# Attention and mixing on one core, eight batches in flight by steps: row units in two groups a step, value products between column units, one dense unit last

## The chip, the cores and the metric

The kernel runs on one core of a Trainium2 chip. The metric is the device time of one execution in microseconds, the median of several; lower is better.

## The reference

The input x is 8 batches of 1024 tokens with 256 channels. Each batch has six modulation vectors sa, ca, ga, sb, cb, gb from a small conditioning input. All is float32.

```
h = layernorm(x) * (1 + ca) + sa
q, k, v = split(h @ w_in.T)                       # 16 heads of 16 channels
a = softmax(causal(q @ k.T / 4)) @ v
x = x + ga * (a @ w_out.T + b_out)
h = layernorm(x) * (1 + cb) + sb
p = h shifted by one token
r = sigmoid((mu_r*h + (1-mu_r)*p) @ W_r.T)
k = relu((mu_k*h + (1-mu_k)*p) @ W_k.T) ** 2
out = x + gb * (r * (k @ W_v.T))
```

## The kernel before

Products that need float32 accuracy are made of a high and a low part (`o_hi`, `o_lo` and so on; three matmuls for one). Queries and keys are split into three bfloat16 parts that lie stacked in the partitions of `q_stack` and `k_stack`, one pair of stacks for even and one for odd groups of heads.

**Batches, quarters, steps.** A batch `b` has G = 4 quarters `s` of 4 heads, a quarter has 12 steps `t`. Three parts of three batches run beside one another: the attention of batch b, the front of batch b+1 (layernorm, transposes, q, k and v) and the back of batch b-1 (everything behind the attention, 256 tokens a quarter). `body(b, kind)` is written once for each engine; kinds are first (only a front), start, second, mid (a loop), last and drain (only backs). `timeline` yields for each step the back items `(b, s, u)`, where u is the stage number from 0 to `BACK_END`-1; a stage past 11 falls in the next quarter. In the drain a quarter's back starts `TAIL_LAG` = 5 steps after the one before it. Each engine runs its own program in order and waits on semaphores.

**Column units.** `score_columns` makes transposed scores, keys in the partitions, of one key tile against up to 512 queries; a unit fills one of 3 banks `col_ps`, and ScalarE's `exps` turns it into `weights`. A quarter has 38 of them: 4, 4, 2, 1, 4, 4, 4, 4, 4, 4, 2, 1 by step. On the steps with the diagonal (0 to 3 and 8 to 11) GpSimd's `select` zeroes the masked part. `values` multiplies the weights of step t with `v_ones`; TensorE does it in step t+1.

**Row units.** The exponent needs each query's maximum beforehand. `row_unit` makes the scores of the next group of heads with queries in the partitions, in one of 3 banks `row_ps`, and VectorE's `maximum` reduces it. A quarter has 38 row units and, at two points, a transpose of the split maxima (`mt0` for the first half of the queries, `MT1` for the second), which SyncE copies into a row of `q_stack`. `PER_STEP` says how many units of `ORDER` a step has. The first 11 need the first half of the next stack, the others its second half; SyncE's `fill_stacks` writes these with 6 DMAs a side. The second half's query side is released by the last column unit of the quarter before, its key side comes after `place_values` (which waits for ScalarE's `val_out` copy) and the three DMAs of MT1's maxima.

**Dense units.** All other products share a single bank `dense_ps`: v, qk and transposed (front), and out, norm, recept, key and value (back). `V_STEPS`, `QK_STEPS`, `T_STEPS` and `BACK_STEPS` say on which step TensorE runs each. `claim_dense` lets the next one start when the one before has been taken out of the bank (semaphores `free[...]`): v, transposed, norm, recept and key by ScalarE, out and value by VectorE, qk by both.

**Order within a step, before.** TensorE: column units, then (at step 0) MT1 of the quarter before, the value product of the step before, the front unit, the back units; the row units are spread among them by `rows_after`, in proportion to a weight of 1 to 4 for columns, 4 for a value product and 6 for a dense unit. VectorE: a fifth of the maxima, back items, front items, three fifths of the maxima, `rest_of_qk`, a fifth of the maxima. ScalarE: half of the exps, back items, the other exps, copies of `val_ps`, front unit. GpSimd: select, front, back.

The back's stages before, by engine: att_n (VectorE 0), o_hi (ScalarE 1), the residual add and o_lo (GpSimd 1), out (TensorE 2), gated and x1 (VectorE 3), stats (4), rstd (GpSimd 4), xn_c (VectorE 5), norm (TensorE 5), h (ScalarE 6), h_diff (GpSimd 6), mixed (VectorE 7), mix_hi (ScalarE 8), mix_lo (GpSimd 8), recept and key (TensorE 9 and 10, emptied by ScalarE at 10 and 11), k_hi (ScalarE 11), k_lo (GpSimd 11), value (TensorE 13), mix_out (VectorE 14), the output's two adds and its DMA (GpSimd 14).

## Time and profile before

| | |
|---|---|
| median of 3 runs | 1716.88 us (1710.48 to 1721.14) |
| the profiled execution | 1714.77 us |
| its span | 1713.2 us |
| TensorE matmuls (PE) | busy 1425.7 us, 83% of the span |
| VectorE (DVE) | 1183.1 us, 69% |
| ScalarE (ACT) | 910.8 us, 53% |
| GpSimd (POOL) | 738.0 us, 43% |
| mean granted TensorE clock | 0.958 of full speed |

The span lies within the execution's time, 1.6 us of which is around it. PEld is TensorE's loading of weights, which overlaps its matmuls; SPq is SyncE's DMA queue. A matmul's end is modelled, so a busy TensorE is not one at its peak. Idle time of an engine is put down to what released it last; "issue" means that the profile shows no releaser.

### The profile page before, as it was taken

The numbers are of one execution on the slowest core, as the hardware profiler recorded it, in microseconds if no ns is written. First come the engines' busy times: TensorE is split into PE (matmuls) and PEld (weight loads), VectorE is DVE, ScalarE is ACT, GpSimd is POOL, SyncE is SP. The second block draws the span as 40 slices with busy tenths as digits, with TensorE's granted clock in tenths as the row PEclk, the third lists the DMA queues.
The fourth block names the chain that finished last, engine by engine and source line by source line (L and its number), as shares of the span: only waits on it lengthen the run. The fifth ranks groups of instructions, "written<-read, shape, count | busy, mean of one in ns | idle before, by whom it ended". The sixth has DMA issues, their size and how long they took to land.

```text
span 1713.2 us, 33031 instructions
## 1 busy us (share of the span) xinstructions
PE 1425.7 (83%) x10024; PEld 749.3 (44%) x10024; DVE 1183.1 (69%) x2306; ACT 910.8 (53%) x1795; POOL 738.0 (43%) x878
## 2 busy tenths in 40 slices
PE   3698999788988988788897888879888898899755
PEld 2253444344544444444443445434454444444344
DVE  4768767877677776877578675777767777777232
ACT  2057555556555555565455555565545655566521
POOL 3223314444354434455344443545435553444554
PEclk9899999999999999999999999999999999999855
DMA  3211131111311122111311113111221112111200
GB/s 105 63 62 52 49 105 57 38 54 55 104 57 47 49 72 85 43 53 57 93 55 48 45 57 96 64 42 45 72 86 56 55 49 78 47 61 40 71 19 19
DMA packets 101874, 103.00 MB, mean 60 GB/s; under 512 B 21296, under 2 KB 89912, under 8 KB 101696
## 3 DMA queue, kind: packets, MB, share of 16 engines
q1 hardware_dynamic: 98176, 91.59, 16.6%
q0 software_dynamic: 2560, 8.39, 1.3%
q8 instruction: 94, 1.54, 0.4%
q10 hardware_dynamic: 960, 0.79, 0.2%
q14 instruction: 84, 0.69, 0.1%
HBM read 31.74 MB, written 8.94 MB: 24 GB/s over the span
## 4 chain that ended last, share of the span: by engine, by line
PE 47%; DVE 21%; issue 12%; ACT 9%; POOL 6%; SPq 2%; DMA 2%; DVEq 1%; ACTq 0%; POOLq 0%
PE row_ps L1076 9%; PE val_ps L1100 9%; PE col_ps L1046 7%; PE dense_ps L1110 7%; DVE max_a L871 7%; PE dense_ps L1112 5%; PE dense_ps L1111 5%; ACT weights L715 4%; DVE mixed L984 3%; DVE max_b L871 2%; PE row_ps L1081 2%; PE dense_ps L1129 2%; DVE xn_c L910 2%; DVE gated L968 1%; SPq L459 1%
## 5 line engine op out<-in xcount | busy, mean ns | idle before, releaser
L715 ACT ACTIVATE weights<-col_ps 128x512 f32<-128x512 f32 (+1 forms) x1216 | 620.6, 580 | 471.1 <-PE col_ps L1046 469.1
L871 DVE TENSOR_REDUCE max_a<-row_ps 128x1 f32<-128x512 f32 (+3 forms) x864 | 550.3, 663 | 224.7 <-PE row_ps L1081 145.4
L1076 PE MATMUL row_ps<-k_stack,q_stack 125*128 125x512 bf16 (+3 forms) x1536 | 460.5, 337 | 54.7 <-DVE max_a L871 35.3
L1046 PE MATMUL col_ps<-q_stack,k_stack 128*128 128x512 bf16 (+3 forms) x1536 | 393.9, 333 | 57.1 <-ACT weights L715 36.0
L597 POOL TENSOR_SCALAR_AFFINE_SELECT weights<-weights 128x512 f32<-128x512 f32 x256 | 169.5, 662 | 533.0 <-ACT weights L715 531.1
L1100 PE MATMUL val_ps<-weights,v_ones 128*32 128x512 f32 (+3 forms) x3072 | 329.5, 501 | 16.4 <-POOL weights L597 15.6
L1076 PEld LDWEIGHTS row_ps<-k_stack,q_stack 125*128 125x128 bf16 x1536 | 144.9, 99 | 348.8 <-DVE max_a L871 173.0
L871 DVE TENSOR_REDUCE max_b<-row_ps 128x1 f32<-128x384 f32 (+3 forms) x352 | 213.1, 635 | 107.3 <-PE row_ps L1081 106.9
L1046 PEld LDWEIGHTS col_ps<-q_stack,k_stack 128*128 128x128 bf16 x1536 | 131.9, 98 | 220.8 <-ACT weights L715 138.8
L1081 PE MATMUL row_ps<-causal,ident_bf 128*128 128x128 bf16 x1024 | 203.6, 224 | 0.0
L1081 PEld LDWEIGHTS row_ps<-causal,ident_bf 128*128 128x128 bf16 x1024 | 102.9, 100 | 14.3
L1100 PEld LDWEIGHTS val_ps<-weights,v_ones 128*32 128x32 f32 x3072 | 60.8, 108 | 109.4 <-issue 66.1
L984 DVE SCALAR_TENSOR_TENSOR mixed<-h_diff,mus,h 128x256 f32<-128x256 f32 x128 | 76.2, 654 | 21.8 <-POOL h_diff L652 21.7
L659 POOL TENSOR_TENSOR mix_lo<-mixed,mix_hi 128x512 fp32r<-128x512 f32 x64 | 81.4, 1291 | 6.8 <-ACT mix_hi L782 6.8
L652 POOL TENSOR_TENSOR h_diff<-h 128x512 f32<-128x512 f32 x32 | 33.3, 1039 | 92.9 <-ACT h L774 92.2
L1110 PE MATMUL dense_ps<-h_hi,w_hi 128*128 128x512 f32 x128 | 60.8, 475 | 7.9 <-DVE qk_rest L942 4.2
L1110 PE MATMUL dense_ps<-w_hi,o_hi 128*128 128x256 f32 x128 | 41.2, 322 | 26.7 <-POOL o_lo L638 20.2
L1129 PE MATMUL dense_ps<-ident,xn_c 128*128 128x128 f32 x128 | 22.5, 303 | 47.6 <-DVE xn_c L910 45.5
L723 ACT ACTIVATE val_out<-val_ps 128x512 f32<-128x512 f32 x64 | 38.6, 603 | 30.9 <-PE val_ps L1100 30.7
L1110 PE MATMUL dense_ps<-mix_hi,w_hi 128*128 128x256 f32 x128 | 40.9, 320 | 15.0 <-ACT h_hi L758 12.1
L736 ACT ACTIVATE v_ones<-dense_ps 128x512 f32<-128x512 f32 x32 | 20.1, 629 | 60.5 <-PE dense_ps L1112 60.5
L1112 PE MATMUL dense_ps<-h_hi,w_lo 128*128 128x512 f32 x128 | 51.0, 399 | 0.0
(128 smaller groups left out, 2261.1 us busy)
## 6 DMA issues: line engine op xcount, KB each, us to landing
q_stack<-q_part SPq DMA_DIRECT2D x384, 64.0 KB, 2.5
k_stack<-k_part SPq DMA_DIRECT2D x372, 64.0 KB, 2.5
xa<-in_x SPq DMA_DIRECT2D x8, 1024.0 KB, 6.9
att<-val_out SPq DMA_DIRECT2D x64, 128.0 KB
recips<-recip_rows SPq DMA_DIRECT2D x32, 256.0 KB
xq<-in_x SPq DMA_DIRECT2D x28, 256.0 KB, 3.3
out<-xq POOLq DMA_DIRECT2D x28, 256.0 KB, 2.6
q_stack<-max_rows SPq DMA_DIRECT2D x192, 4.0 KB
```

What stands on the lines that cost most here:

```text
L597: nc.gpsimd.affine_select(out=w, in_=w, compare_op=ALU.is_ge, fill=0.0, base=0, pattern=[[0, G], [1, P]], channel_multiplier=-1).then_inc( ...
L659: nc.gpsimd.tensor_tensor(mix_lo[:, m], mixed[:, m], mix_hi[:, m].bitcast(F32), ALU.subtract).then_inc(mix_lo_done, 1)
L715: nc.scalar.activation(weights[:, t % 2, h:h + n, 0:q1 - q0], col_ps[bank][:, 0:n * (q1 - q0)].rearrange("p (h q) -> p h q", h=n), ACT.Exp ...
L871: nc.vector.reduce_max(dest, bank[:, 0:len(heads) * (k1 - k0)].rearrange("p (h k) -> p h k", h=len(heads)), AX_X).then_inc(max_done, 1)
L984: last = nc.vector.scalar_tensor_tensor(mixed[:, m, c, :], h2_diff[:, c, :], mus[:, m, c:c + 1], h2[s % 2][:, c, 0:QT], ALU.mult, ALU.add)
L1046: last = nc.tensor.matmul(col_ps[bank][:, i * (q1 - q0):(i + 1) * (q1 - q0)], k_stack[s % 2][:, h, P * j:P * (j + 1)], q_stack[s % 2][:, h ...
L1076: last = nc.tensor.matmul(bank[:, n * width:(n + 1) * width], q_stack[stack][0:MAX_AT, h, P * i:P * (i + 1)], k_stack[stack][0:MAX_AT, h, ...
L1081: last = nc.tensor.matmul(bank[:, (n + 1) * width - P:(n + 1) * width], ident_bf[:], causal[:], start=False, stop=end, skip_group_check=True)
L1100: last = nc.tensor.matmul(val_ps[32 * h:32 * h + 32, q0 - base:q1 - base], v_ones[:, j, G * s + h].rearrange("p d a -> p (d a)"), weights[ ...
L1110: nc.tensor.matmul(dst, a_hi(c), b_hi(c), start=(c == 0), stop=False)
L1111: nc.tensor.matmul(dst, a_hi(c), b_lo(c), start=False, stop=False)
L1112: last = nc.tensor.matmul(dst, a_lo(c), b_hi(c), start=False, stop=(c == KC - 1))
```

## The change

- TensorE's step becomes: two row units, half of the column units, the value product of the step before, the other column units, the remaining row units, then the front's and the back's dense unit. MT1 moves from step 0 of the next quarter to the end of step 11. `rows_after` and its weights go.
- `PER_STEP` puts 4, 4, 3, 4, 5, 2, 4, 4, 2, 4, 2, 1 units in the steps instead of 2, 3, 3, 3, 3, 4, 4, 5, 5, 4, 2, 1, and `mt0` stands behind 19 row units instead of 14.
- The front's and the back's units get other steps, so that a step holds one dense unit (two in step 1 of a batch's first quarter). norm, recept and key are one step later.
- ScalarE and VectorE empty the dense bank at the head of the next step, by `empty_dense` (and `front`, `rest_of_qk` with t - 1). What splits a value in a high part comes last in ScalarE's step (`split`). VectorE does one half of mixed before its later maxima and one after; its other back items and the front come last.
- GpSimd does the front and back items of a step ahead of the select; its stages are 2, 5, 8, 10, 13 and 15 instead of 1, 4, 6, 8, 11 and 14. At stage 2 o_lo comes ahead of the residual add. `BACK_END` is 16 instead of 15.

```diff
-PER_STEP = [2, 3, 3, 3, 3, 4, 4, 5, 5, 4, 2, 1]
+PER_STEP = [4, 4, 3, 4, 5, 2, 4, 4, 2, 4, 2, 1]
-V_STEPS, QK_STEPS, T_STEPS = (0, 1, 2, 3), (4, 6, 7, 8), (4, 6, 8, 10)
+V_STEPS, QK_STEPS, T_STEPS = (0, 1, 3, 9), (4, 5, 7, 8), (3, 5, 7, 9)
-BACK_STEPS = dict(zip(BACK_UNITS, (2, 5, 9, 10, 13)))
-BACK_END = 15
+BACK_STEPS = dict(zip(BACK_UNITS, (2, 6, 10, 11, 13)))
+BACK_END = 16
...
+        def row_groups(t):
+            first = sum(PER_STEP[:t])
+            units = list(range(first, first + PER_STEP[t]))
+            return units[:2], units[2:]
...
 # gpsimd
             def body(b, kind):
                 for s, t, at in timeline(b, kind):
-                    if attends(kind) and t in DIAGONAL:
-                        select(b, s, t)
                     front(b, kind, s, t)
                     for item in at:
                         back(*item)
+                    if attends(kind) and t in DIAGONAL:
+                        select(b, s, t)
...
 # scalar
             def body(b, kind):
                 for s, t, at in timeline(b, kind):
-                    units = range(COL_FIRST[t], COL_FIRST[t + 1]) if attends(kind) else ()
-                    for c in units[:len(units) // 2]:
-                        exps(b, s, t, c)
+                    front(b, kind, s, t)
                     for item in at:
-                        back(*item)
-                    for c in units[len(units) // 2:]:
+                        empty_dense(*item)
+                    for c in range(COL_FIRST[t], COL_FIRST[t + 1]) if attends(kind) else ():
                         exps(b, s, t, c)
...
-                    front(b, kind, s, t)
+                    for item in at:
+                        split(*item)
...
 # vector
+                    early, late = row_groups(t) if has_rows(kind, s) else ([], [])
                     if t == 0 and attends(kind):
                         maximum(b, s - 1, MT1)
-                    for u in units[0]:
+                    for u in early[:1]:
+                        maximum(b, s, u)
+                    rest_of_qk(b, kind, s, t)
+                    for item in at:
+                        empty_dense(*item)
+                    for u in early[1:]:
                         maximum(b, s, u)
                     for item in at:
+                        mix(*item, 0)
+                    for u in late:
+                        maximum(b, s, u)
+                    for item in at:
+                        mix(*item, 1)
                         back(*item)
                     front(b, kind, s, t)
-                    for u in units[1] + units[2] + units[3]:
-                        maximum(b, s, u)
-                    rest_of_qk(b, kind, s, t)
-                    for u in units[4]:
-                        maximum(b, s, u)
...
 # tensor
+                    for u in early:
+                        row_unit(b, s, u)
+                    for c in cols[:len(cols) // 2]:
                         score_columns(b, s, t, c)
-                        if t:
-                            rows_after(COL_HEADS[t])
-                    if t == 0 and cols:
-                        row_unit(b, s - 1, MT1)
-                        rows_after(4)
-                    if has_values:
-                        values(*late)
-                        rows_after(4)
+                    if attends(kind) if t else has_late(kind, s):
+                        values(*last)
+                    for c in cols[len(cols) // 2:]:
+                        score_columns(b, s, t, c)
+                    for u in late:
+                        row_unit(b, s, u)
                     if unit:
                         claim_dense()
                         front(unit)
-                        rows_after(6)
-                    for item in backs_now:
-                        claim_dense()
-                        back(*item)
-                        rows_after(6)
-                    rows_after(work)
+                    for item in at:
+                        if back_unit(*item):
+                            claim_dense()
+                            back(*item)
+                    if t == STEPS - 1 and has_rows(kind, s):
+                        row_unit(b, s, MT1)
```

## Rows read from the trace of the kernel before

**Rows 1.** The page, its chain of work that ended last, by engine.

```profile
PE 47%; DVE 21%; issue 12%; ACT 9%; POOL 6%; SPq 2%; DMA 2%; DVEq 1%; ACTq 0%; POOLq 0%
```

**Rows 2.** Busy time by stretch: batch 0, batches 1 to 6, batch 7, drain.

```profile
core 0: us, PE busy (x) PEld busy (x) DVE busy (x) ACT busy (x) POOL busy (x), PEclk, DMA share, GB/s
90.60:246.20 155.60, 143.12 (x1043) 64.18 (x1042) 114.83 (x230) 95.34 (x189) 42.91 (x60) 0.98 0.16 52
246.20:1448.70 1202.50, 1037.21 (x7479) 540.83 (x7478) 879.30 (x1718) 677.50 (x1346) 541.21 (x645) 0.98 0.19 62
1448.70:1616.20 167.50, 147.05 (x1078) 73.12 (x1076) 105.53 (x206) 98.71 (x196) 73.69 (x87) 1.00 0.17 52
1616.20:1713.20 97.00, 51.39 (x228) 45.04 (x228) 28.81 (x55) 21.06 (x37) 51.89 (x52) 0.56 0.09 31
```

**Rows 3.** The same view, batch 3 by quarter.

```profile
642.70:696.10 53.40, 48.43 (x346) 27.02 (x344) 36.14 (x67) 28.31 (x57) 23.68 (x28) 1.00 0.24 75
696.10:750.00 53.90, 41.23 (x301) 20.41 (x300) 42.87 (x90) 32.13 (x67) 25.45 (x32) 0.97 0.14 46
750.00:798.00 48.00, 43.62 (x312) 22.70 (x315) 34.86 (x67) 26.75 (x54) 24.59 (x28) 1.00 0.16 53
798.00:846.20 48.20, 40.98 (x297) 20.75 (x296) 32.48 (x65) 25.63 (x52) 17.10 (x20) 0.93 0.24 76
```

**Rows 4.** Who waited for whom, PE's matmuls, batch 3 (us, times, longest).

```profile
PE dense_ps L1129 <- DVE xn_c L910: 5.9, 4, 2.7
PE row_ps L1076 <- DVE max_a L871: 4.8, 5, 1.6
PE col_ps L1046 <- ACT weights L715: 4.6, 7, 1.3
PE col_ps L1046 <- issue: 3.6, 1, 3.6
PE val_ps L1100 <- POOL weights L597: 2.1, 2, 1.8
PE dense_ps L1110 <- ACT h_hi L758: 2.0, 1, 2.0
PE dense_ps L1110 <- ACT v_ones L736: 1.0, 2, 0.6
PE dense_ps L1110 <- DVE mix_out L992: 0.9, 3, 0.5
```

**Rows 5.** Instructions in order of time, batch 4, quarter 2, steps 3 and 4.

```profile
903.44 3.82 SPq L459 DMA_DIRECT2D k_stack<-k_part  x6
...
906.53 0.38 PE L1046 MATMUL col_ps<-q_stack,k_stack 128*128 128x128 bf16 x4
...
909.13 0.39 PE L1076 MATMUL row_ps<-k_stack,q_stack 125*128 125x512 bf16 x1
...
910.84 0.66 POOL L597 TENSOR_SCALAR_AFFINE_SELECT weights<-weights 128x512 f32<-128x512 f32 x1
...
911.55 0.42 PE L1100 MATMUL val_ps<-weights,v_ones 128*32 128x128 f32 x8 [1.75 <-POOL weights L597]
```

**Rows 6.** Instructions in order of time, the drain, one turn of its loop.

```profile
1668.90 1.26 POOL L636 TENSOR_TENSOR weights<-weights,gates_att 128x512 f32<-128x512 f32 x1
...
1668.97 3.66 DVE L984 SCALAR_TENSOR_TENSOR mixed<-h_diff,mus,h 128x256 f32<-128x256 f32 x4 [3.96 <-POOL h_diff L652]
...
1670.11 1.44 POOL L638 TENSOR_TENSOR o_lo<-att_n,o_hi 128x512 fp32r<-128x512 f32 x1
...
1671.70 0.55 PE L1110 MATMUL dense_ps<-w_hi,o_hi 128*128 128x256 f32 x1 [5.82 <-POOL o_lo L638]
...
1672.71 2.51 POOL L659 TENSOR_TENSOR mix_lo<-mixed,mix_hi 128x512 fp32r<-128x512 f32 x2 [1.16 <-ACT mix_hi L782]
```

**Rows 7.** DMA issues: KB each, median us from issue to landing.

```profile
k_stack<-k_part SPq DMA_DIRECT2D x372, 64.0 KB, 2.5
```

**Rows 8.** VectorE's mixed (whole run) and residual add (batch 3): ns min/median/max.

```profile
L984 DVE SCALAR_TENSOR_TENSOR mixed<-h_diff,mus,h x128: 470/477/1541, 274.9 to 1691.3; 128x256 f32<-128x256 f32 x128
L971 DVE TENSOR_TENSOR xq<-xq,gated x4: 693/988/1408, 656.3 to 806.9; 128x512 f32<-128x512 f32 x4
```

More of the change, by code:

```diff
@@ L405, in build @@
         BEFORE = {"start": "first", "second": "start", "mid": "second", "last": "mid", "drain": "last"}
-        def gaps(t):
-            first, n = sum(PER_STEP[:t]), PER_STEP[t]
-            out = [[] for _ in range(5)]
-            for k in range(n):
-                out[k * 5 // n].append(first + k)
-            return out
+        def row_groups(t):
+            first = sum(PER_STEP[:t])
+            units = list(range(first, first + PER_STEP[t]))
+            return units[:2], units[2:]
         def residual(bb, s):
@@ L761, in front, with empty_dense @@
                     last.then_inc(free["transposed"], 1)
[L763 removed]
+            def empty_dense(b, s, u):
                 q = quarters(b, s)
[L765 to L769 removed]
+                if u == 7:
                     act.wait_ge(ready["norm"], q + 1)
@@ L776, in back, with split @@
                     last.then_inc(free["norm"], 1)
-                if u == 8:
+                if u == 11:
+                    act.wait_ge(ready["recept"], q + 1)
+                    wait(act, free["value"], q)
+                    nc.scalar.activation(recept[:], dense_ps[:], ACT.Tanh, scale=0.5).then_inc(free["recept"], 1)
+                if u == 12:
+                    act.wait_ge(ready["key"], q + 1)
+                    nc.scalar.activation(k_relu[:], dense_ps[:], ACT.Relu).then_inc(free["key"], 1)
+            def split(b, s, u):
+                q = quarters(b, s)
+                if u == 1:
+                    act.wait_ge(att_done, b * 2 - (1 if s < 2 else 0))
+                    wait(act, ready["out"], q)
+                    nc.scalar.activation(o_hi[:], att_n[:, :, QT * s:QT * (s + 1)], ACT.Copy).then_inc(o_hi_done, 1)
+                if u == 9:
                     wait(act, ready["key"], q)
@@ L949, in reciprocals, with empty_dense, mix @@
                 nc.vector.reciprocal(sums[half][:], sums[half][:]).then_inc(recip_done, 1)
+            def empty_dense(b, s, u):
+                q = quarters(b, s)
+                if u == 3:
+                    dve.wait_ge(ready["out"], q + 1)
+                    if s == 0:
+                        dve.wait_ge(gates_att_in, b * 16)
+                    ga = gates_att[:, 0:1, :].broadcast_to([P, 2, D])
+                    nc.vector.tensor_tensor(gated[:], dense_ps[:], ga, ALU.mult).then_inc(free["out"], 1)
+                if u == 14:
+                    dve.wait_ge(ready["value"], q + 1)
+                    wait(dve, out_done, q)
+                    nc.vector.scalar_tensor_tensor(mix_out[:], recept[:], 1.0, dense_ps[:], ALU.add, ALU.mult
+                                                   ).then_inc(free["value"], 1)
+            def mix(b, s, u, m):
+                q = quarters(b, s)
+                if u == 8:
+                    if m == 0:
+                        dve.wait_ge(diff_done, q + 1)
+                        wait(dve, mix_lo_done, q * 2)
+                    for c in range(KC):
+                        last = nc.vector.scalar_tensor_tensor(
+                            mixed[:, m, c, :], h2_diff[:, c, :], mus[:, m, c:c + 1],
+                            h2[s % 2][:, c, 0:QT], ALU.mult, ALU.add)
+                    last.then_inc(mixed_done, 1)
             def back(b, s, u):
```

85 lines of the change are left out of this document (22 added, 63 removed).

## Prediction

> **What bounds the kernel now.** I read the profile from the whole to the step. First the chain of work that ended last [rows 1]: TensorE holds 47% of it, VectorE 21%, and 12% is issue, so there is no single full engine. Then the stretches of the span [rows 2], cut where the first value product of a batch starts: setup and the first batch's front end at 90.6 us, batch 0 takes 155.6 us, the six batches in which every part runs take 1202.5 us (200.4 each), the last takes 167.5 us, and the drain, in which only the back stages of one batch are left, 97.0 us. The reader should see that TensorE is busy 1037.2 of the 1202.5 us: a steady batch has 20 to 30 us in which TensorE has nothing it may start. Then one steady batch by quarter [rows 3]: 203.5 us with 174.3 busy, 29.2 idle. Its second quarter is the one that stands out: 53.9 us although TensorE's busy time there (41.2) is that of the fourth quarter (41.0, in 48.2 us). What it has more is VectorE (42.9 against 32.5 us) and ScalarE (32.1 against 25.6 us): the layernorm and the transposes of the next batch. Time is lost there in the order, not in an amount of matrix work.
>
> Last, what TensorE waited for in that batch [rows 4]. The normalised residual of the "norm" unit: 5.9 us, 4 times, once a quarter. The one dense bank, not yet emptied: 2.0 + 1.0 + 0.9 = 3.9 us. The banks of row and column units, not yet reduced or exponentiated: 4.8 + 4.6 = 9.4 us. A select on GpSimd: 2.1 us. One wait of 3.6 us has no releaser, and I leave it where it is.
>
> **The change, part by part, in one steady batch.** No computing instruction is added or removed; the number of column units, row units, dense units and copies is the same. So every term is a wait.
>
> (a) "norm" moves from step 5 to step 6, while VectorE still writes its input in the step numbered 5. It gets nearly a step (about 4 us: 200.4 us over 48 steps) against waits of at most 2.7 us [rows 4]. I take all 5.9 us.
>
> (b) One dense unit a step, at its end; its bank is emptied first thing in ScalarE's next step and after one maximum on VectorE, while TensorE runs two row units and half the columns. Before, three steps of a batch hold two dense units (value with v, out with v, key with the last transposes); after, only step 1 of the first quarter does. Of 3.9 us one wait stays, at the 0.5 us of a v_ones wait (1.0 us in 2): -3.4 us. What hides the emptying is the row pair and the columns; without that cover the 3.9 us would be back.
>
> (c) Row units come two at the start of a step and the rest at its end, with three row banks; column units in two halves with the value product between. Before, single row units stand after single columns, so one late maximum holds the columns behind it, and ScalarE behind these. Ends: 0 (the waits only move) and -9.4 us. I take half, -4.7 us: VectorE has the same number of maxima to do, and only their being out of step with TensorE is mended.
>
> (d) GpSimd now does the front and back items of a step and then the select; before, the select came first. Queued behind the items is the select, and behind it the value product of the next step and all that TensorE has after it. At step 3 the old order comes to the same, as the output's work stands at the end of step 2: in the second quarter of batch 4 the select starts at 910.84 and TensorE's value product stands idle for 1.75 us until 911.55 [rows 5]. The other quarters show no such wait. The output's two adds (1.26 us each, as the add of the same size [rows 6]) and its DMA issue stay directly ahead of that select. New are o_lo and the residual add ahead of the select of step 2, and two mix_lo (2.51 us [rows 6]) ahead of that of step 10. The value product comes a whole row pair, and half the columns, into the following step, which hides 2 to 4 us. Ends 0 and +16.3 us (below, rival 3); I take +2.
>
> (e) The second half of the row units needs the next stack's second half. It is the 12th row unit, in step 4 before (8 + 3 units through step 3) and now the 12th comes at the head of step 3, ahead of that step's columns. In quarter 2 of batch 4 the k_stack fill is issued from 903.44 to 907.26, and a fill lands 2.5 us after issue [rows 5, 7], so near 909.1: TensorE's row unit starts at 909.13, and step 3's columns were at 906.53. Asked for at 906.5 it would wait 2.6 us: ends 0 and +10.4 us (four quarters). Against it: SyncE's own chain starts sooner. The fill's first half is released by the last column unit, now ahead of the key unit and of the last transpose; the value product that val_out waits for now stands after half of step 0's columns, not after all of them; and three more row units stand ahead. The one thing that goes the other way is att_n at the end of VectorE's step 0. I take +2.
>
> Sum of a steady batch: -5.9 - 3.4 - 4.7 + 2 + 2 = -10.0 us of TensorE idleness. Not all of it is time: where VectorE carries the chain (21% to TensorE's 47% [rows 1]) the end doesn't move. I take three quarters, -7.5 us. The batches at the ends are costed by their idle time against 29.2: batch 0 has 155.6 - 143.1 = 12.5 us, the last 167.5 - 147.0 = 20.5 us [rows 2], together 1.13 batches. So 7.13 x -7.5 = -53.5 us.
>
> (f) The drain. Here one loop of dense unit, emptying, dense unit is walked once per quarter. Before, "out" waits 5.82 us for GpSimd's residual add and o_lo [rows 6]; after, o_lo comes first and a step earlier against the dense units, which takes that wait from the loop. But the output's two adds and its DMA issue (about 3.3 us) now stand ahead of the next quarter's mix_lo (first 1.26 us) in the same step, and the recept unit waits for that; norm and key move one step and the drain has one step more (16 stages to a quarter, before 15). -5.8 + 3.3 + 1.3 and about 3 for the step added to the chain gives some +2 a quarter at most; over the drain I take +5 us, ends -8 and +12.
>
> Total -53.5 + 5 = -48.5. The profiled execution took 1714.8 us (span 1713.2 and 1.6 around it), 2.1 under the median of the three runs. Forecast 1714.8 - 48.5 = 1666 us.
>
> **A rule against the trace.** The four mixed instructions take 477 ns at the median and 1541 ns at the most [rows 8], and in the drain they need 3.66 us in a row while GpSimd runs o_lo and the residual add [rows 6]. The Trainium skill, SBUF — State Buffer, section "SBUF: two separate sides", says that a VectorE operation with two SBUF inputs and a GpSimd operation exclude each other for a whole instruction; by that rule, the trace agrees. The change puts the residual's add (693 ns at the least, 988 at the median [rows 8]) beside the output's two adds in step 3, and takes the drain's mixed instructions away from o_lo. By the rows that is +0.3 to +0.7 us a quarter in the first place and up to -1.8 in the second, some +10 us in all at worst, since neither is on TensorE's path as a rule; I leave both out of the sum.
>
> **The rivals.**
> 1. More of the waits go. All of (c), nothing for (d) and (e): -18.7, three quarters of it -14.0, x 7.13 = -100, +5: 1620 us. For it: the second quarter has 5.7 us over the fourth at the same matrix work. Against: VectorE must keep up in pairs. Chance 0.15.
> 2. The fill takes the place of what was removed: (e) at its full 10.4 us, so -1.6 a batch, -11 and +5: 1708 us, a band of 1690 to 1732. It decides if the last k_stack fill lands later than step 3 begins. For it: the row unit starts just as the fill lands [rows 5]. Against: SyncE's head start. Chance 0.20.
> 3. Slower: GpSimd's items ahead of the select. If the last exp of a step is followed by less than the items' time before the value product, TensorE stops as at 911.55. At the wait of 2.1 us for the three quarters that have none (6.3) and a mix_lo pair of 2.51 us in four (10.0) that is 16.3 a batch in place of the +2: +4.3, x 7.13 = +31, +5: 1751 us. For it: the one measured case. Against: the half set of columns now placed ahead of the value product. Chance 0.14.
> 4. It doesn't do what it says: VectorE is late for the row pairs everywhere, and the order of TensorE makes no difference. 1715 us, chance 0.03.
>
> **How the numbers follow.** Forecast 0.48, with its own range 1640 to 1690. Below 1610 lies about 0.06 (of rival 1), above 1735 about 0.11 (of rival 3), so the range is 1610 to 1735. One per cent of the time before is 17 us, about what a measurement can tell from no change. Faster by more: 0.48 + 0.15 + 0.04 of rival 2 = 0.67; within 1%: 0.16 + 0.03 = 0.19; slower: 0.14.
>
> **What would show it.** In the waits of TensorE: norm <- xn_c gone (a); dense <- h_hi, v_ones, mix_out near 0.5 us a batch (b); row and column waits about halved (c); value <- select no more than some 4 us a batch (d), and if it is 10 or more, rival 3 holds; a row unit idle at the head of step 3 until a k_stack fill lands: under 1 us a quarter, rival 2 if 2 us. Steady batches near 193 us, the second quarter under 50; the drain near 102. The prediction is wrong if the waits go and the batches stay at 200: then VectorE's own sequence is the bound and the three quarters of the sum are the bad step.

## The result and the profile after

The changed kernel takes 1751.51 us (median of 4 runs, 1749.64 to 1753.62) against 1719.01 us of the kernel before (median of 4, 1710.48 to 1731.40). The ratio is 1.0184 with a 95% interval of 1.0118 to 1.0249: slower by 1.8%, where 1666 us was forecast. The profiled execution took 1749.64 us, its span 1748.0 us, 34.8 more than before.

First the same stretches as in [rows 2], cut where the first value product of batch 0, 1 and 7 and the last one start: batch 0, the six full batches, the last batch, the drain.

```profile
96.80:274.20 177.40, 146.12 (x1027) 65.30 (x1040) 115.77 (x231) 97.26 (x189) 42.94 (x60) 0.95 0.14 44
274.20:1471.50 1197.30, 1025.57 (x7393) 536.24 (x7477) 901.45 (x1717) 693.35 (x1345) 536.92 (x645) 0.98 0.20 62
1471.50:1643.00 171.50, 147.49 (x1063) 72.95 (x1075) 107.98 (x205) 100.38 (x195) 73.23 (x87) 0.97 0.16 51
1643.00:1748.00 105.00, 44.57 (x228) 39.01 (x228) 25.30 (x55) 22.46 (x40) 51.57 (x52) 0.68 0.09 30
```

The loss is not where most of the work is. The six full batches take 199.5 us each, before 200.4 [rows 2]: 5.2 us won in all. Batch 0 takes 177.4 for 155.6 us (+21.8), the last batch 171.5 for 167.5 (+4.0), the drain 105.0 for 97.0 (+8.0), and all ahead of batch 0's first value product 96.8 for 90.6 (+6.2). These add up to +34.8. TensorE was granted a clock of 0.95 in batch 0, before 0.98, and of 0.68 in the drain, before 0.56.

Next what TensorE's matmuls waited for in a full batch, the one from 670.5 to 872.1 us, to be held against [rows 4]; us, times, longest.

```profile
PE row_ps L1090 <- DVE max_a L871: 11.0, 16, 3.4
PE row_ps L1090 <- DMA k_stack<-k_part: 4.5, 3, 1.8
PE row_ps L1090 <- issue: 3.6, 1, 3.6
PE col_ps L1060 <- ACT weights L712: 2.3, 6, 0.8
PE val_ps L1114 <- POOL weights L594: 1.9, 2, 1.0
PE dense_ps L1124 <- POOL mix_lo L656: 1.2, 2, 0.9
PE dense_ps L1124 <- POOL o_lo L627: 0.9, 1, 0.9
PE dense_ps L1124 <- ACT v_ones L733: 0.7, 1, 0.7
```

No row names xn_c, and the dense bank's rows (v_ones, qk_rest, gated) are small. In their place stand the row banks and a DMA, the k_stack fill.

One trap in reading it: the page lists 9913 matmuls and 10024 weight loads, and of the 1536 column matmuls 1425 have a record. A wait ahead of a matmul without a record is missing from this view, and that matmul's own time counts as idle. The weight loads are all there, but they run ahead under other matmuls, so a load can wait while TensorE is busy: in the batch of [rows 4] columns wait 17.8 us for ScalarE by weight loads and 4.6 us by matmuls. The traces of the kernel before and of a_out_last (below; the changed kernel with another order in the drain only) have all 10024 matmuls, and these two are compared here, over the six full batches. Before, 1202.5 us:

```profile
PE dense_ps L1129 <- DVE xn_c L910: 36.7, 24, 3.0
PE row_ps L1076 <- DVE max_a L871: 28.8, 30, 1.7
PE col_ps L1046 <- ACT weights L715: 28.5, 45, 1.3
PE val_ps L1100 <- POOL weights L597: 12.4, 12, 1.8
PE dense_ps L1110 <- ACT h_hi L758: 12.1, 6, 2.0
...
PE row_ps L1076 <- DMA k_stack<-k_part: 1.0, 4, 0.3
```

With the change (a_out_last), 1197.2 us:

```profile
PE row_ps L1090 <- DVE max_a L871: 59.3, 87, 3.4
PE row_ps L1090 <- DMA k_stack<-k_part: 33.9, 19, 4.9
PE val_ps L1114 <- POOL weights L594: 11.7, 12, 1.2
...
PE col_ps L1060 <- ACT weights L712: 8.9, 18, 0.7
...
PE dense_ps L1124 <- POOL mix_lo L656: 7.4, 13, 1.0
PE dense_ps L1124 <- POOL o_lo L627: 5.8, 6, 1.0
```

A batch is a sixth of these. norm's 6.1 us are gone, and columns wait 3.3 us less for ScalarE. Rows wait 5.1 us more for VectorE's maxima and 5.5 us more for the fill, and dense units wait 2.0 us more for a low part from GpSimd (mix_lo, o_lo and k_lo, 15.2 us for 3.4 over the six). TensorE idles 26.9 us a batch, before 27.5.

In batch 0, which has no back, the same comparison shows where the time went. Before:

```profile
PE row_ps L1076 <- DMA k_stack<-k_part: 7.3, 3, 2.6
PE col_ps L1046 <- ACT weights L715: 3.5, 7, 0.9
```

With the change (a_out_last, batch 0 176.6 us):

```profile
PE row_ps L1090 <- DMA k_stack<-k_part: 13.5, 3, 4.7
PE val_ps L1114 <- POOL weights L594: 8.0, 7, 1.6
PE row_ps L1090 <- DVE max_a L871: 4.5, 13, 0.9
PE col_ps L1060 <- ACT weights L712: 1.6, 3, 0.7
```

The fill costs 6.2 us more, the value products behind the select 8.0 us and the maxima 4.5 us, where the kernel before has no such rows. TensorE is idle for 30.2 us, before 12.5, and busy 3.3 us longer at the lower clock. The select in its turn stands behind ScalarE's exps: GpSimd waits 103.2 us for them in the changed kernel's batch 0, before 72.8.

The DMA row is the 12th row unit. In batch 0's third quarter, in order of time:

```profile
187.41 1.91 SPq L531 DMA_DIRECT2D q_stack<-max_rows  x3
...
189.51 3.82 SPq L456 DMA_DIRECT2D k_stack<-k_part  x6
...
191.47 0.63 POOL L594 TENSOR_SCALAR_AFFINE_SELECT weights<-weights 128x512 f32<-128x512 f32 x1 [2.03 <-ACT weights L712]
195.14 1.03 PE L1090 MATMUL row_ps<-k_stack,q_stack 125*128 125x512 bf16 x2 [4.19 <-DMA k_stack<-k_part]
...
197.76 0.60 ACT L712 ACTIVATE weights<-col_ps 128x512 f32<-128x512 f32 x1 [6.46 <-PE col_ps L1060]
```

The reader should see who pays: the row unit at the head of step 3 idles TensorE for 4.2 us, and ScalarE, whose columns stand behind it, 6.5 us.

### The profile page after: what moved, and what is told of

It is laid out like the page before. It is cut to its first block, busy times and chain, and to the rows that moved or that the text cites. A ratio compares the mean times of both kernels' runs of the same rounds, so it can differ in the third digit from the quotient of the medians.

```text
span 1748.0 us, 32941 instructions
## 1 busy us (share of the span) xinstructions
PE 1416.2 (81%) x9913; PEld 742.8 (42%) x10024; DVE 1206.8 (69%) x2306; ACT 931.0 (53%) x1795; POOL 733.0 (42%) x878
## 4 chain that ended last, share of the span: by engine, by line
PE 46%; DVE 18%; issue 11%; POOL 7%; ACT 7%; SPq 6%; DMA 2%; another core or an unknown queue 2%; DVEq 0%; ACTq 0%; POOLq 0%
PE val_ps L1114 11%; PE col_ps L1060 10%; PE row_ps L1090 8%; DVE max_a L871 7%; PE dense_ps L1124 6%; PE dense_ps L1126 5%; PE dense_ps L1125 4%; ACT weights L712 4%; SPq L456 3%; POOL mix_lo L656 2%; DMA k_stack<-k_part 2%; PE row_ps L1095 2%; DVE max_b L871 1%; SPq L531 1%
## 5 line engine op out<-in xcount | busy, mean ns | idle before, releaser
L712 ACT ACTIVATE weights<-col_ps 128x512 f32<-128x512 f32 (+1 forms) x1216 | 632.8, 579 | 499.6 <-PE col_ps L1060 395.3
L1090 PE MATMUL row_ps<-k_stack,q_stack 125*128 125x512 bf16 (+3 forms) x1536 | 430.5, 342 | 151.9 <-DVE max_a L871 73.2
L1060 PE MATMUL col_ps<-q_stack,k_stack 128*128 128x512 bf16 (+3 forms) x1425 | 358.1, 332 | 23.4 <-ACT weights L712 15.4
L1060 PEld LDWEIGHTS col_ps<-q_stack,k_stack 128*128 128x128 bf16 x1536 | 114.9, 99 | 311.4 <-ACT weights L712 199.9
L1114 PEld LDWEIGHTS val_ps<-weights,v_ones 128*32 128x32 f32 x3072 | 61.4, 109 | 173.9 <-issue 102.6
L975 DVE SCALAR_TENSOR_TENSOR mixed<-h_diff,mus,h 128x256 f32<-128x256 f32 x128 | 62.1, 546 | 28.6 <-POOL h_diff L649 28.6
L1124 PE MATMUL dense_ps<-w_hi,mix_hi 128*128 128x256 f32 x128 | 42.0, 328 | 33.9 <-POOL mix_lo L656 33.3
L660 POOL TENSOR_TENSOR k_lo<-k_sq,k_hi 128x512 fp32r<-128x512 f32 x32 | 43.0, 1345 | 43.4 <-ACT k_hi L795 43.4
L866 DVE COPY max_rows<-row_ps 12x512 bf16<-12x512 bf16 x64 | 26.1, 407 | 44.3 <-PE row_ps L1080 24.8
L752 ACT ACTIVATE h_full<-dense_ps,mod_front 128x256 f32<-128x256 f32 x64 | 32.6, 562 | 43.1 <-PE dense_ps L1143 38.6
L1124 PE MATMUL dense_ps<-w_hi,k_hi 128*128 128x256 f32 x128 | 39.7, 310 | 19.1 <-POOL k_lo L660 13.2
```

What stands on the lines that cost most here:

```text
L712: nc.scalar.activation(weights[:, t % 2, h:h + n, 0:q1 - q0], col_ps[bank][:, 0:n * (q1 - q0)].rearrange("p (h q) -> p h q", h=n), ACT.Exp ...
L975: last = nc.vector.scalar_tensor_tensor(mixed[:, m, c, :], h2_diff[:, c, :], mus[:, m, c:c + 1], h2[s % 2][:, c, 0:QT], ALU.mult, ALU.add)
L1060: last = nc.tensor.matmul(col_ps[bank][:, i * (q1 - q0):(i + 1) * (q1 - q0)], k_stack[s % 2][:, h, P * j:P * (j + 1)], q_stack[s % 2][:, h ...
L1090: last = nc.tensor.matmul(bank[:, n * width:(n + 1) * width], q_stack[stack][0:MAX_AT, h, P * i:P * (i + 1)], k_stack[stack][0:MAX_AT, h, ...
L1114: last = nc.tensor.matmul(val_ps[32 * h:32 * h + 32, q0 - base:q1 - base], v_ones[:, j, G * s + h].rearrange("p d a -> p (d a)"), weights[ ...
L1124: nc.tensor.matmul(dst, a_hi(c), b_hi(c), start=(c == 0), stop=False)
```

## The experiments

All ratios are against the kernel before, run beside each on the same chip; that kernel's medians in the three sets were 1720.6, 1727.1 and 1727.8 us. "Stretches" are those above, from each profiled execution. Waits are those of TensorE's matmuls where nothing else is said; a_spread, a_out_last, d_mix and d_fill_sooner have all matmul records, as has the kernel before; the others lack 111 to 118. The theories: A, the fill took the place of what was removed, with A' for MT1; B, grouping columns and the value product makes TensorE wait for ScalarE; C, GpSimd's items hold the select; D, the drain's order on GpSimd.

| run | us | ratio (95%) | batch 0 | full batch | last | drain |
|---|---|---|---|---|---|---|
| before | 1719.0 | | 155.6 | 200.4 | 167.5 | 97.0 |
| changed | 1751.5 | 1.0184 (1.0118 to 1.0249) | 177.4 | 199.5 | 171.5 | 105.0 |
| a_fill_late | 1734.4 | 1.0101 (1.0048 to 1.0154) | 173.7 | 196.4 | 169.5 | 107.2 |
| a_mt1_back | 1734.7 | 1.0102 (1.0062 to 1.0141) | 177.7 | 196.3 | 173.5 | 108.2 |
| a_both | 1723.3 | 1.0016 (0.9985 to 1.0047) | 172.2 | 196.2 | 171.2 | 107.8 |
| b_rows_early | 1776.3 | 1.0338 (1.0289 to 1.0387) | 167.3 | 206.7 | 174.0 | 96.9 |
| a_select_first | 2136.1 | 1.2371 (1.2322 to 1.2419) | 196.3 | 253.1 | 217.1 | 106.1 |
| c_values_late | 1750.5 | 1.0142 (1.0102 to 1.0182) | 174.8 | 200.5 | 166.8 | 107.8 |
| c_spread | 1716.7 | 0.9947 (0.9919 to 0.9975) | 158.3 | 199.1 | 162.7 | 108.6 |
| c_out_last | 1700.6 | 0.9840 (0.9800 to 0.9880) | 172.8 | 196.4 | 170.2 | 84.9 |
| a_out_last | 1733.2 | 1.0034 (1.0005 to 1.0063) | 176.6 | 199.5 | 173.0 | 87.0 |
| a_spread | 1724.3 | 0.9979 (0.9954 to 1.0004) | 170.7 | 197.4 | 162.9 | 108.0 |
| d_mix | 1687.2 | 0.9774 (0.9735 to 0.9813) | 158.2 | 196.7 | 161.5 | 93.5 |
| d_fill_sooner | 1685.5 | 0.9751 (0.9713 to 0.9789) | 157.1 | 197.5 | 163.5 | 90.6 |

**a_fill_late.** The changed kernel, with its 12th row unit in step 4.

```diff
-PER_STEP = [4, 4, 3, 4, 5, 2, 4, 4, 2, 4, 2, 1]
+PER_STEP = [3, 3, 3, 2, 5, 4, 4, 5, 3, 4, 2, 1]
```

> The changed kernel with 3, 3, 3, 2, 5, 4, 4, 5, 3, 4, 2, 1 row units a step, so that the first unit that needs the stack's second half stands in step 4 again, and not at the head of step 3. Theory A (the stack fill took the place of what was won): the idle time ahead of that unit, 4.6 to 5.8 us a quarter in batch 0 and some 6 us a steady batch in the changed kernel, falls under 1 us each; batch 0 comes back by 12 us or more, steady batches by 5, the whole to 1700 us or less. Theory B (columns in pairs make TensorE wait for ScalarE, and the fill wait only takes the place of other waiting): the idle time ahead of the unit goes, but column and value waits grow, and the whole stays within 12 us of 1751.

A full batch became 3.1 us shorter and batch 0 3.7. The sign is A's, the size a third of what A expected in batch 0: there the value product now waits where the row unit did. Over the six full batches the fill's wait fell from 34.0 to 6.3 us and the rows' behind max_a from 60.6 to 42.4, while value behind select rose from 11.7 to 61.4; in batch 0 the fill's fell from 13.7 to 6.0 and value behind select rose from 8.0 to 12.6. A is right about the wait and wrong that it was the whole.

**a_mt1_back.** The changed kernel, with MT1 as before in step 0.

```diff
+                    if t:
+                        for u in early:
+                            row_unit(b, s, u)
                     for c in cols[:len(cols) // 2]:
                         score_columns(b, s, t, c)
+                    if t == 0:
+                        if attends(kind):
+                            row_unit(b, s - 1, MT1)
+                        for u in early:
+                            row_unit(b, s, u)
...
-                    if t == STEPS - 1 and has_rows(kind, s):
-                        row_unit(b, s, MT1)
```

> The changed kernel with MT1, the transpose of the last split maxima, back in step 0 of the next quarter, behind the first half of its columns (and the row pair behind it), and not at the end of step 11. Theory A': at the end of step 11 it waits for VectorE's last maximum and split, 1.5 to 2 us, with all columns of the next quarter queued behind; back in step 0, batch 0 and the last batch gain 4 to 8 us each and the whole 10 to 20 us. Theory B: columns wait for ScalarE instead, no change beyond 8 us.

Right in the sum (16.8 us) and wrong in the place: batch 0 didn't move (177.7), the last batch got 2.0 us longer, a full batch 3.2 us shorter, and the stretch before batch 0 took 92.8 us for 96.8, with its first column matmul at 85.8 us for 92.0. (In the kernel before it starts at 84.2.) The edit does two things, since the row pair of step 0 also goes behind the first columns; they were not tried apart.

**a_both.** Both edits.

```diff
-PER_STEP = [4, 4, 3, 4, 5, 2, 4, 4, 2, 4, 2, 1]
+PER_STEP = [3, 3, 3, 2, 5, 4, 4, 5, 3, 4, 2, 1]
...
+                    if t == 0:
+                        if attends(kind):
+                            row_unit(b, s - 1, MT1)
...
-                    if t == STEPS - 1 and has_rows(kind, s):
-                        row_unit(b, s, MT1)
```

> Both edits together: the row units a step of the first edit and MT1 behind the first columns of step 0. Theory A with A': the gains add up, 1690 us or less, below the kernel before. Theory B: 1730 us or more.

Neither A nor B: 1723.3 us is between their numbers. In a full batch both edits together give what each gives alone (196.2 against 196.4 and 196.3), so there their gains don't add. In batch 0 they give 5.2 us together; most of its loss stays.

**b_rows_early.** The kernel before, with the changed numbers of row units.

```diff
-MT0_AFTER = 3
+MT0_AFTER = 8
-PER_STEP = [2, 3, 3, 3, 3, 4, 4, 5, 5, 4, 2, 1]
+PER_STEP = [4, 4, 3, 4, 5, 2, 4, 4, 2, 4, 2, 1]
```

> The kernel before with the changed kernel's row units a step (4, 4, 3, 4, 5, 2, 4, 4, 2, 4, 2, 1, mt0 behind 19) and nothing else. Theory A: the unit that needs the stack's second half comes a step early here too and waits for the fill; 10 to 25 us slower than before, most of it in batch 0. Theory B: the spread order keeps columns going ahead of that unit; within 8 us of before.

Both theories fell short: it costs 55.7 us, more than the whole change. Batch 0 has 11.7 us of it, the full batches 6.3 each. So the distribution of row units is a loss by itself, and in a full batch the rest of the change makes up for it. Its 11.7 us in batch 0 are over half of the changed kernel's 21.8, and the fill's wait, 11.8 us for 7.3, is 4.5 of it. No single wait carries the 6.3 us: over the full batches rows behind max_a rose by 19.0 us, columns behind ScalarE by 12.4, dense units behind gated and mix_out by 13.5 and rows behind the fill by 5.6, while norm's fell by 15.9 (its trace lacks 111 column matmuls). What these share wasn't tried.

**a_select_first.** The changed kernel with GpSimd's order of before.

```diff
+                    if attends(kind) and t in DIAGONAL:
+                        select(b, s, t)
                     front(b, kind, s, t)
                     for item in at:
                         back(*item)
-                    if attends(kind) and t in DIAGONAL:
-                        select(b, s, t)
```

> The changed kernel with GpSimd's select ahead of the step's front and back items again. Theory C (rival 3 of the prediction: the items hold the select, and with it the value product): value waits go down by 5 us or more a steady batch, the whole to 1735 us or less. Theory B' (the value product waits for ScalarE's exps, which come late since half the columns stand behind the value product before): batch 0, which has no back items, keeps its 177 us, the steady batches gain nothing, and since h_diff, mix_lo and o_lo come later the whole is 1751 to 1790 us.

C is refuted and turned round: a full batch takes 253.1 us. With the select first GpSimd waits for the step's exps before it makes the operand of that step's own dense unit. Over the full batches:

```profile
PE dense_ps L1124 <- POOL mix_lo L656: 87.0, 24, 4.6
PE dense_ps L1124 <- POOL o_lo L627: 65.6, 24, 3.6
PE dense_ps L1124 <- POOL k_lo L660: 48.3, 23, 2.4
```

In the changed kernel these three are 15.0 us together. Value behind select stayed where it was, 11.5 us for 11.7. Of the 321 us that the full batches lost, 119 are TensorE's longer busy time, at a granted clock of 0.87 for 0.98. Items first is a part of the change that the rest cannot do without.

**c_values_late.** a_both, with the value product behind all columns.

```diff
-                    if attends(kind) if t else has_late(kind, s):
-                        values(*last)
                     for c in cols[len(cols) // 2:]:
                         score_columns(b, s, t, c)
+                    if attends(kind) if t else has_late(kind, s):
+                        values(*last)
```

> The two edits of a_both, and besides TensorE's value product behind all columns of the step instead of between the halves; nothing else moves. Theory B': from the last column of a step to its value product there were only the late rows, a row pair and half the columns, in batch 0 without dense units 1.5 us against 2.2 us of exps and 0.65 us of select; a value product behind all columns takes 10 us or more off batch 0 (172 us) and 3 or more off the last batch, 1708 us or less in all. Theory B'' (it is the columns standing close that hold TensorE, not the place of the value product): column waits go up by what value waits go down, within 8 us of 1723.

Theory B' fell. In batch 0 most of the value waits went (13.5 us behind the select, now 2.4), columns now waited, 8.6 us behind ScalarE for 1.2, and batch 0 became 2.6 us longer. A full batch became 4.3 us longer: over the six, value behind select fell from 59.5 to 3.3 us and columns behind ScalarE rose from 3.2 to 88.5. B'' has the mechanism, but not its number, as the whole is 27 us above 1723. With groups, the value product between the halves was well placed; moving one kind behind another only moves the waits.

**c_spread.** a_both, with rows and columns in turn.

```diff
-                    for c in cols[:len(cols) // 2]:
-                        score_columns(b, s, t, c)
...
+                    units = early + late
+                    for n, c in enumerate(cols):
+                        score_columns(b, s, t, c)
+                        if t and units:
+                            row_unit(b, s, units.pop(0))
+                    if t == 0 and attends(kind):
+                        row_unit(b, s - 1, MT1)
+                    for u in units[:1]:
+                        row_unit(b, s, u)
+                    if attends(kind) if t else has_late(kind, s):
+                        values(*last)
+                    for u in units[1:]:
+                        row_unit(b, s, u)
```

> The two edits of a_both, and besides TensorE's rows and columns in turn (a column, a row, and so on), then the value product, then the remaining rows, then the dense unit. Theory B'': the time between columns lets ScalarE keep up, column waits (28 us a batch) halve, batch 0 returns to 158 us or less, the whole to 1700 or less. Theory B': the same as with the value product alone behind the columns, within 8 us of that run.

B'' holds for batch 0 (158.3 from 172.2, where 158 or less was expected) and the last batch (162.7 from 171.2), and not for a full batch, which got 2.9 us longer, nor for the whole (1716.7, expected 1700 or less). Nor did the column waits halve, as it said: in batch 0 3.2 us for 1.2 (by weight loads 25.2 for 22.2). What went is value behind select, 13.5 to 1.7 us. c_values_late has its value product as late and the rows and columns in groups: against it, taking them in turn gives 16.5 us in batch 0. The two in turn with the value product between the columns wasn't run. Over the full batches no value product waits for the select any more (59.5 us in a_both; 9.1 us behind ScalarE instead), but columns behind ScalarE rose from 3.2 to 32.7 us and rows behind max_a from 41.4 to 62.2. One reading, not shown: the dense unit that ends each step there is already the pause in which the other engines catch up. It isn't a rule even for this kernel, since on the changed kernel alone the same order makes a full batch shorter (a_spread).

**c_out_last.** a_both, with the output's work last in GpSimd's step.

```diff
-                    for item in at:
+                    for item in sorted(at, key=lambda item: item[2] == 15):
                         back(*item)
```

> The two edits of a_both, and besides GpSimd's output work (stage 15, two adds and the DMA issue) behind the other items of its step. Theory D (the drain's extra 8 to 11 us are the recept unit waiting for mix_lo behind the output work): the drain falls from 107.8 to 98 us or less, the rest stays, 1714 us. Rival: the added step and the later norm and key lengthen the drain's loop whatever GpSimd does first; drain at 105 us or more.

D holds, by more than expected: drain 84.9 for 107.8 us, everything else in place. In the changed kernel's drain, in order of time:

```profile
1703.58 1.26 POOL L668 TENSOR_TENSOR mix_out<-mix_out,gates_mix 128x512 f32<-128x512 f32 x1 [2.98 <-DVE mix_out L964]
1704.92 1.26 POOL L670 TENSOR_TENSOR weights<-weights,mix_out 128x512 f32<-128x512 f32 x1
1706.48 0.80 POOL L672 DMA_DIRECT2D out<-weights  x1 [0.30 <-POOL weights L670]
1707.31 2.50 POOL L656 TENSOR_TENSOR mix_lo<-mixed,mix_hi 128x512 fp32r<-128x512 f32 x2
...
1708.73 0.55 PE L1124 MATMUL dense_ps<-w_hi,mix_hi 128*128 128x256 f32 x1 [7.57 <-POOL mix_lo L656]
```

An output that nobody waits for stands ahead of mix_lo, and TensorE idles 7.6 us for it. TensorE's waits for mix_lo in the drain fell from 22.5 to 10.4 us. Part of the 22.9 us comes with the clock: it was granted at 0.63 in a_both's drain and 0.79 in this one, and TensorE's busy time there is 50.2 and 38.1 us. Shorter idle stretches and a higher clock come together here; that doesn't say which caused which.

**a_out_last.** The same edit on the changed kernel alone.

```diff
-                    for item in at:
+                    for item in sorted(at, key=lambda item: item[2] == 15):
                         back(*item)
```

> The changed kernel with GpSimd's output work (stage 15) behind the other items of its step, and nothing else. Only in the drain does stage 15 share a step with others. Theory D: the 22.9 us that this gave on top of a_both belong to the order alone, so the drain falls from 105 to some 83 us here too and the whole to 1729 us; batches as in the changed kernel. Rival: it helped only with a_both's timing; less than 12 us.

D holds without a_both: drain 87.0 for 105.0, full batches 199.5 as in the changed kernel. TensorE's wait for mix_lo in the drain, changed kernel and then this one:

```profile
PE dense_ps L1124 <- POOL mix_lo L656: 25.4, 4, 7.7
```

```profile
PE dense_ps L1124 <- POOL mix_lo L656: 10.4, 4, 4.2
```

**a_spread.** Rows and columns in turn on the changed kernel alone (the rows of c_spread's edit, with MT1 left at the end of step 11).

```diff
-                    for u in early:
-                        row_unit(b, s, u)
-                    for c in cols[:len(cols) // 2]:
+                    units = early + late
+                    for n, c in enumerate(cols):
                         score_columns(b, s, t, c)
+                        if units:
+                            row_unit(b, s, units.pop(0))
+                    for u in units[:1]:
+                        row_unit(b, s, u)
                     if attends(kind) if t else has_late(kind, s):
                         values(*last)
-                    for c in cols[len(cols) // 2:]:
-                        score_columns(b, s, t, c)
-                    for u in late:
+                    for u in units[1:]:
                         row_unit(b, s, u)
```

> The changed kernel with TensorE's rows and columns in turn, then the value product, then the remaining rows, and nothing else (MT1 and the row units a step as changed). Theory B'': batch 0 falls from 177 to 165 us or less, the last batch by 5 or more, steady batches within 3 us of 199.5: 1720 to 1735 us. Theory A: what batch 0 lost is the fill and MT1, batch 0 stays above 172.

The whole is in the range that B'' named (1724.3) and a full batch 2.1 us shorter, within its 3. Batch 0 fits neither: 170.7 us is above the 165 of B'' and below the 172 of A. a_both's edits alone give 5.2 us there, turn by turn alone 6.7, all three 19.1 (177.4 to 158.3). Each hides a part of the other: with the rows in turn, MT1 at the end of step 11 waits 6.0 us in batch 0 for its split maxima, and the fill still costs 13.5. Over the full batches the fill's wait is 20.9 us for 34.0, rows behind max_a 40.6 for 60.6, and columns behind ScalarE 43.8 for 13.2.

**d_mix.** c_out_last, with c_spread's order when `kind in ("start", "last")` and the groups otherwise.

```diff
+                    if kind in ("start", "last"):
+                        units = early + late
+                        for n, c in enumerate(cols):
+                            score_columns(b, s, t, c)
+                            if t and units:
+                                row_unit(b, s, units.pop(0))
...
+                    else:
+                        if t:
+                            for u in early:
+                                row_unit(b, s, u)
+                        for c in cols[:len(cols) // 2]:
+                            score_columns(b, s, t, c)
```

> a_both, the output work last in the drain, and TensorE's rows and columns in turn in batch 0 and the last batch only, where a front or a back is missing; steady batches keep the groups. If the parts add up: 1700.6 - 14 (batch 0) - 8 (last batch) = 1678 us. Rival: with a loop body in another order than the batch before, what is won in batch 0 is paid back in batch 1; 1690 or more.

1687.2 us, 2.3% below the kernel before (0.9735 to 0.9813). Batch 0 and the last batch kept what c_spread gave (158.2 and 161.5) and the full batches stayed at 196.7, so the rival of a payback is out. The drain was 93.5 us and not 84.9, at a granted clock of 0.59 against 0.79; there the sum misses its 9 us.

**d_fill_sooner.** d_mix, with SyncE's key side of the second half issued ahead of MT1's maxima.

```diff
                     if attends(kind):
+                        if has_rows(kind, s):
+                            fill_stacks(b, s + 1, 1, (1,))
                         hold(max_done, unit_index(b, s - 1, MT1) + 1)
...
-                        if has_rows(kind, s):
-                            fill_stacks(b, s + 1, 1, (1,))
```

> d_mix, and besides SyncE issues the key side of the stack's second half ahead of the three DMAs of MT1's maxima (1.9 us), with the wait for these behind it. Theory A: the wait of the 12th row unit for the fill, 2 to 3 us a quarter in batch 0 and 0.5 in a steady one, is on the path; 5 to 10 us less than d_mix. Rival: VectorE's maxima catch up anyway; within 4 us.

1.7 us, inside its noise: the rival. In batch 0 the fill's wait (7.5 us in d_mix) went, and the columns that need the maxima took it over:

```profile
PE col_ps L1060 <- DMA q_stack<-max_rows: 6.5, 3, 2.2
```

Fill and maxima share SyncE's queue, and moving one ahead makes the other late. It doesn't show that d_mix's rows would gain nothing from a fill that were sooner at no one's cost.

## Why the prediction was wrong

Two steps of the sum failed, about equally: what a full batch would win, and that the ends of the run would win in proportion. Against the forecast the full batches are 39.8 us too long, the ends and the stretch before them 40.5, the drain 3.0. With only one of the first two wrong the time would have been some 1706 to 1710 us. First the terms of a full batch, by the matmul waits above.

(a) Right. norm's wait for xn_c, 6.1 us a batch [rows 4: 5.9], has no row after.

(b) Right in kind, a little small in size. The bank's waits (h_hi, v_ones, mix_out, gated) were 4.0 us a batch and are 1.3 (v_ones, qk_rest, gated): 2.7 us won, 3.4 forecast. Put at nothing were the dense units' own waits for mix_lo, o_lo and k_lo, which GpSimd now makes in other steps: they grew by 2.0 us.

(c) This term failed. It took -4.7 us from rows and columns together, with ends of 0 and -9.4. They wait 1.8 us more: columns 3.3 less, rows 5.1 more. The range left out that a group can be worse than single units; I had reasoned from three row banks and not asked what stands between the last column of a step and its value product. c_values_late and c_spread both have the value product behind the columns, and differ in whether rows and columns come in groups or in turn: in batch 0 that is worth 16.5 us.

(d) Right to be small in a full batch: value behind select, 2.1 us before, is 2.0. In batch 0 it is 8.0 us, before none. Rival 3 named 1751 us, the time that was measured, by luck: the 16.3 us a batch behind the select that it is made of are nowhere, a_select_first shows that its opposite costs 385 us, and it was taken whole, where the forecast took three quarters of its terms (by that, rival 3 would have said 1743 us).

(e) Too small. The wait is there as described: +5.5 us a batch, where +2 was taken and 10.4 was the end. SyncE's head start didn't cover it. Nor is its removal all gain: a_fill_late takes it out and gets 3.1 us back, as the value products wait in its place. In batch 0 it is 13.5 us for 7.3.

**The full batches**: -10.0 us of idle time each and -45 us in all (6 times -7.5) forecast, -0.6 of idle time and -5.2 us in all measured. The terms come to -6.1 - 2.7 + 2.0 + 1.8 - 0.1 + 5.5 = +0.4. The three quarters that turned idle time into time were not the fault, as the idle time itself did not fall. What left norm and the dense bank came back at the rows, the fill and GpSimd's low parts. a_fill_late or a_mt1_back return 3 of the 7.5 us.

**The ends of the run** are the other step. I costed batch 0 and the last as 1.13 full batches at the same gain, -8.5 us; they gave +25.8, and the stretch before batch 0, which I left out, +6.2. A batch without a back (or a front) has nothing for (a) to win, or little, and no back's dense units (or front's) between its groups, so less time passes for the fill and for ScalarE. That is argued from the order; what is shown are the waits and that other orders return the time. Idle time measures how much is lost, not whether this change returns it. Of batch 0's 21.8 us three edits return 19.1 (c_spread). In the stretch before it the edit of a_mt1_back returns 4.0 of the 6.2 us (92.8 for 96.8). The other runs on the changed kernel have 96.5 to 98.0 us with MT1 at the end of step 11 and 92.6 to 94.2 with it back, but for c_values_late (97.3), where the value product that marks the cut stands behind all columns. The granted clock there (0.72, before 0.92) doesn't explain it, as a_fill_late has 98.0 us at 0.95. The rest stays open.

(f) The sign was right, +8.0 for +5, and the mechanism, mix_lo behind the output's work, was described. TensorE's waits for o_lo in the drain, 16.0 us, went as forecast. The price was too low: I weighed 3.3 us against the 5.8 won at "out", and the waits for mix_lo went from 2.5 to 25.4 us, up to 7.7 at a time. a_out_last shows that the order costs 18.0 us: without it these waits are 15.0 us less, and TensorE's busy time is 4.3 us less at another granted clock (0.76 for 0.68). The +8.0 flatters the change, as the drain before had its clock at 0.56; six of the runs with this order have 0.60 to 0.63 and take 107.2 to 108.6 us. TensorE's largest wait in the drain before, which went:

```profile
PE dense_ps L1110 <- POOL o_lo L638: 16.0, 3, 5.8
```

**VectorE beside GpSimd.** The mean of the 128 mixed instructions fell from 654 to 546 ns; in the drain, where they no longer run beside o_lo, from 724 to 479, four in 1.67 us where [rows 6] had 3.66. The rule of the Trainium skill, SBUF — State Buffer, section "SBUF: two separate sides", asks for just that; by it, the trace agrees.

```profile
1700.63 1.67 DVE L975 SCALAR_TENSOR_TENSOR mixed<-h_diff,mus,h 128x256 f32<-128x256 f32 x4 [1.21 <-POOL h_diff L649]
```

That the drain gained by it isn't shown. For the residual's add the prediction had the direction wrong. The kernel before has it beside the output's adds already (in batch 3 one of 1.41 us from 705.09, with an add of GpSimd's from 704.68 to 705.95); with the change its mean over the full batches fell from 977 to 675 ns. And 0.7 us a quarter would have been 22 us at worst, not 10.

## What to carry to other kernels

Cost an edit of the order for each phase of a pipeline by itself: the phases that lack one part (start, end, drain) have less cover, and here they held all of the net loss. Before taking wait time as gain, ask who inherits it. In queues that run in order, with few banks between them, a wait that is taken out at one place came back at the next in most of these runs; in batch 0 taking rows and columns in turn took it out, while in a full batch that helped or hurt with the rest of the order. In a queue that runs in order, put the work that others wait for first and output that nobody waits for last. And before waits of two traces are compared, count the records of each.

## What the runs showed of the hardware that I had not expected

Matmul records were missing in some traces and not in others (1425 of 1536 column matmuls in the changed kernel's), while all 10024 weight loads were there; in the changed kernel's trace the 111 missing ones were all column matmuls. ScalarE's exps show waits for an unknown releaser, 102.4 us in the changed kernel's trace and none in the kernel before's or a_out_last's. And drains of nearly equal work differed in granted clock, 0.56 to 0.79 of full speed, with TensorE's busy time in them between 51.4 and 38.1 us: two drains with the same order (c_out_last 84.9 us, d_mix 93.5) differ by 12.7 us of it, more than by their length.
